# The context's keys laid out by group, and softmax sums spread before they are inverted

## What is computed

```python
# x: (32, 64, 256) after layer norm; ctx: (32, 1601, 256); 16 heads of 16
q = split_heads(x @ Wq.T + bq)
k = split_heads(ctx @ Wk.T + bk)
v = split_heads(ctx @ Wv.T + bv)
score = einsum('bhqd,bhkd->bhqk', q, k) * 4.0
attn = softmax(score, axis=-1)
out = einsum('bhqk,bhkd->bhqd', attn, v) @ Wp.T + bp
```

## Time and profile before

| | us |
|---|---|
| median of three runs | 1734.32 (1733.7 to 1734.82) |
| the profiled execution, its own time | 1735.91 |
| its span, from the first to the last instruction | 1734.1 |
| attention, first scores to last weighting | about 60 to 1240 of the span |
| circuit and feed-forward | about 1240 to 1330 |
| experts | about 1330 to the end |

### The profile page before, as it was taken

The page is one execution under the profiler, slowest core; times in us unless marked ns, Lnnn a source line. Parts: engine busy times, 40 slices in busy tenths (PEclk is TensorE's granted clock), DMA queues, the critical chain, the costliest instruction groups (busy, mean ns, idle before and its releaser), DMA issues. The chain is left out here.

```text
span 1734.1 us, 59228 instructions
## 1 busy us (share of the span) xinstructions
PE 1666.1 (96%) x24340; PEld 1377.8 (79%) x24340; DVE 1425.4 (82%) x3316; ACT 1220.5 (70%) x3297; POOL 948.8 (55%) x1427
## 2 busy tenths in 40 slices
PE   7999999999999999999999999996798899999998
PEld 4777777777777777777777777775577899999998
DVE  5699898998989989898998989888875676767657
ACT  3687788777888778887877878787554365656552
POOL 5265646556465565655556555554310448888850
PEclk9999999999999999999999999996797999999999
DMA  5011111211112111121111111111102356666632
GB/s 177 22 64 46 48 66 42 67 45 53 60 42 68 45 63 50 42 68 45 65 48 45 65 46 64 48 48 57 62 25 86 122 177 228 219 228 219 226 120 103
DMA packets 43439, 147.89 MB, mean 85 GB/s; under 512 B 5680, under 2 KB 25008, under 8 KB 39712
## 3 DMA queue, kind: packets, MB, share of 16 engines
q1 hardware_dynamic: 38416, 130.72, 22.1%
q0 software_dynamic: 4752, 13.38, 2.5%
HBM read 129.79 MB, written 14.16 MB: 83 GB/s over the span
## 5 line engine op out<-in xcount | busy, mean ns | idle before, releaser
L506 ACT ACTIVATE a_probs<-a_probs,a_bias 128x401 f32<-128x401 f32 x1024 | 631.8, 622 | 2.1
L721 DVE TENSOR_SCALAR_CACHE_REDUCE a_probs<-a_pss 128x401 f32<-128x401 f32 x1024 | 526.2, 570 | 56.9 <-PE a_pss L976 42.6
L736 DVE STREAM_TRANSPOSE a_pT<-a_probs 128x1664 f32<-128x1664 f32 x256 | 488.1, 1907 | 61.3 <-PE a_pso L1005 59.8
L976 PE MATMUL a_pss<-a_keys,a_qown 32*32 32x401 f32 x8192 | 273.6, 508 | 2.7 <-issue 1.3
L316 POOL TENSOR_TENSOR a_clo<-a_raw,a_chi 128x416 fp32r<-128x416 f32 x240 | 251.5, 1081 | 0.0
L1005 PEld LDWEIGHTS a_pso<-a_pT,a_v 128*32 128x32 f32 x6656 | 184.5, 112 | 45.7 <-issue 42.8
L1005 PE MATMUL a_pso<-a_pT,a_v 128*32 128x128 f32 x6656 | 202.5, 279 | 3.5 <-ACT a_op L521 2.7
L339 POOL TENSOR_SCALAR a_ex<-a_probs,a_marks 128x4 f32<-128x4 f32 x256 | 75.9, 296 | 220.2 <-ACT a_probs L506 218.1
L1670 PE MATMUL e_psg<-e_xh,e_guh 128*128 128x256 f32 x660 | 189.5, 287 | 5.5 <-DVE e_hl L1416 4.0
L506 ACT ACTIVATION_READ_ACCUMULATOR a_probs<-a_probs,a_bias 128x1 f32 x1024 | 194.5, 190 | 0.0
L1671 PE MATMUL e_psg<-e_xl,e_guh 128*128 128x256 f32 x660 | 186.6, 283 | 0.0
(11 more groups left out here) (253 smaller groups left out, 4288.8 us busy)
## 6 DMA issues: line engine op xcount, KB each, us to landing
a_raw<-in_ctxT SPq DMA_DIRECT2D x60, 832.0 KB, 4.4
f_gur<-in_wgu SPq DMA_DIRECT2D x24, 1408.0 KB, 6.2
f_dr<-in_wd SPq DMA_DIRECT2D x24, 768.0 KB, 4.7
e_big<-ys_scr SPq DMA_DIRECT2D x8, 512.0 KB, 7.0
a_probs<-in_ctxT SPq DMA_DIRECT2D x2, 1664.0 KB, 9.3
a_x<-in_x SPq DMA_DIRECT2D x16, 128.0 KB, 4.4
rows_scr<-f_a SPq DMA_DIRECT2D x8, 256.0 KB, 2.3
rows_scr<-f_a SPq DMA_DIRECT2D x4, 512.0 KB, 3.5
```

Of the source, the lines that this page charges most:

```text
L506: nc.scalar.activation(z, z, ACT.Exp, bias=bias[:, h % 2, at_bias:at_bias + 1], scale=-1.0, accum_out=esum[:, h % 2, j, 2 * e + r:2 * e + ...
L721: nc.vector.tensor_scalar(probs[:, at % RING, j, 0:KG], ps_s[:, j, 0:KG], -SCALE, None, ALU.mult, ALU.min, accum_out=nmax[:, h % 2, at_max ...
L736: nc.vector.transpose(pT[:, turned_slot(h, i)].rearrange("p j k -> p (j k)"), probs[:, at % RING].rearrange("p j k -> p (j k)")).then_inc( ...
L976: mm = nc.tensor.matmul(ps_s[32 * g:32 * g + 32, j, 0:KG], q_own[32 * j:32 * j + 32, n % 2, m, e, 32 * r:32 * r + 32], keys[32 * j:32 * j ...
```

## The change

The host lays each group's keys side by side: group g holds keys g, g+4, g+8, ..., 401 of them in group 0 and 400 in the others (`REAL`), padded to 416. No key is doubled. A key step then multiplies 402 neighbouring columns of the context. The padded length is 13 x 128, and block t of 128 keys for a value step is now every thirteenth column of all four groups, from t on (`t::KT`), 52 bytes apart. Within a group, block t holds keys t, t+13, ..., 31 places of which can be real.

Scores are in the group's own order, so `take_scores` now reads 403 columns in order and writes element (a, t) to place 32t + a of `probs`: neighbouring elements go 128 bytes apart. Columns 400 to 402 of `ps_s` are set once to -1e30 (group 0's scores overwrite the first of them), so that the exponentials of absent keys are 0. `exponentials` works on 13 runs of 31.

The sums need no correction: `less_extra`, `total`, `spread_sums` and `spread` go. POOL lays the 16 sums of each partition on a diagonal (`lay_sums`, 128 x 512), PE multiplies this with a 128 x 32 tile of ones (`totals`, four matmuls of 128 columns right behind `weigh`), DVE inverts all 128 x 128 results into `o_part` (`invert`), and ACT copies the weighted values out in two halves, each times its parity mask. `gather` is as before. The two waits of DVE named above go. In even periods the step of the first quarter moves to the second, and `spread_max` moves behind both steps of the third quarter.

```diff
+KA = 31
+KP = KT * KA
+KM = 402
...
-OWN, DIAG, EXTRA, KEPT, PARITY = slice(0, 2), slice(2, 34), slice(34, 35), slice(35, 36), (slice(36, 68), slice(68, 100))
+REAL = tuple((SK + QK - 1 - g) // QK for g in range(QK))
+ABSENT = -1e30
+OWN, DIAG = slice(0, 2), slice(2, 34)
...
-        plan = [[(n + 1, 2)], [(n + 1, 3), (n + 1, 4)], [(n + 1, 5), (n + 1, 6)], [(n + 1, 7), (n + 1, 8), (n + 1, 9)]]
+        plan = [[], [(n + 1, 2), (n + 1, 3), (n + 1, 4)], [(n + 1, 5), (n + 1, 6)], [(n + 1, 7), (n + 1, 8), (n + 1, 9)]]
...
+        esum, sums_in, ones = sb("a_esum", [P, 2, HALF, 4]), sb("a_sin", [P, HALF, P]), sb("a_ones", [P, 32])
+        o_part = sb("a_op", [P, 2, 4 * SQ])
...
+        by_block = lambda z: z.rearrange("p (t a) -> p t a", a=32)[:, :, 0:KA]
...
-            def less_extra(h, i):
-                at = HALF * h + i
-                e, r = quads(h)[i]
-                pool.wait_ge(exp_done, HALF * (at + 1))
-                if h > 1 and i == 0:
-                    pool.wait_ge(total_filled, h - 1)
-                if at > 0:
-                    pool.wait_ge(sums_ready, at)
-                nc.gpsimd.tensor_scalar(extra[:], probs[:, at % RING, :, KG - 1], mark[:, EXTRA], None, ALU.mult).then_inc(extra_ready, 1)
-                pool.wait_ge(extra_ready, at + 1)
-                nc.gpsimd.tensor_tensor(out=sums[:, h % 2, :, 2 * e + r], in0=esum[:, h % 2, :, 2 * e + r], in1=extra[:], op=ALU.subtract).then_inc(sums_ready, 1)
-            def spread_sums(h):
-                pool.wait_ge(inverse_ready, h + 1)
+            def lay_sums(h):
+                pool.wait_ge(exp_done, HALF * HALF * (h + 1))
                 if h > 0:
-                    pool.wait_ge(sums_filled, h)
-                nc.gpsimd.tensor_tensor(out=sums_in[:].rearrange("p j q b -> p (j q) b"),
-                                        in0=inverse[:].unsqueeze(2).to_broadcast([32, 4 * HALF, 32]),
-                                        in1=mark[0:32, DIAG].unsqueeze(1).to_broadcast([32, 4 * HALF, 32]), op=ALU.mult).then_inc(sums_spread, 1)
+                    pool.wait_ge(totals_filled, h)
+                nc.gpsimd.tensor_tensor(out=sums_in[:].rearrange("p j (q b) -> p (j q) b", b=32),
+                                        in0=esum[:, h % 2].rearrange("p j q -> p (j q)").unsqueeze(2).to_broadcast([P, 4 * HALF, 32]),
+                                        in1=mark[:, DIAG].unsqueeze(1).to_broadcast([P, 4 * HALF, 32]), op=ALU.mult).then_inc(sums_laid, 1)
...
+                if h > 0:
+                    lay_sums(h - 1)
                 if h > 1:
                     gather(h - 2)
-                less_extra(h, 0)
                 if h % 4 == 1 and h > 4:
...
-                less_extra(h, 1)
-                if n + 2 < B:
                     ctx_low(n + 2, k, raw[:])
-                if h > 0:
-                    spread_sums(h - 1)
-                less_extra(h, 2)
                 if k == 1 and n + 2 < B:
                     own_queries(n + 2)
-                less_extra(h, 3)
...
+                if i == 0 and h > 1:
+                    act.wait_ge(sums_laid, h - 1)
                 for j in some:
-                    z = probs[:, at % RING, j, 0:KG]
+                    z = by_block(probs[:, at % RING, j])
                     at_bias = HALF * i + j
                     nc.scalar.activation(z, z, ACT.Exp, bias=bias[:, h % 2, at_bias:at_bias + 1], scale=-1.0,
...
-                act.wait_ge(sums_filled, h + 1)
+                act.wait_ge(inverse_ready, h + 1)
                 if h > 1:
                     act.wait_ge(o_ready, h - 1)
-                nc.scalar.copy(o_part[:, h % 2, :], ps_o[:, 0:2 * P]).then_inc(o_copied, 1)
+                for e in range(2):
+                    last = nc.scalar.activation(o_part[:, h % 2, SQ * e:SQ * (e + 1)], ps_o[:, SQ * e:SQ * (e + 1)], ACT.Identity, scale=mark[:, e:e + 1])
+                last.then_inc(o_copied, 1)
...
-                    dve.wait_ge(sums_ready, at - RING + 1)
                     dve.wait_ge(turned, at - RING + 1)
...
-                    nc.vector.tensor_scalar(probs[:, at % RING, j, 0:KG], ps_s[:, j, 0:KG], -SCALE, None,
+                    nc.vector.tensor_scalar(by_block(probs[:, at % RING, j]).rearrange("p t a -> p a t"), ps_s[:, j, 0:KP].rearrange("p (a t) -> p a t", t=KT), -SCALE, None,
                                             ALU.mult, ALU.min, accum_out=nmax[:, h % 2, at_max:at_max + 1]).then_inc(max_ready, 1)
...
-                dve.wait_ge(total_filled, h + 1)
-                if h > 0:
-                    dve.wait_ge(sums_spread, h)
-                nc.vector.reciprocal(inverse[:], ps_s[0:32, 0, W:W + 4 * HALF]).then_inc(inverse_ready, 1)
+                dve.wait_ge(totals_filled, h + 1)
+                if h > 1:
+                    dve.wait_ge(o_scaled, h - 1)
+                nc.vector.reciprocal(o_part[:, h % 2, P:2 * P], ps_o[:, P:2 * P]).then_inc(inverse_ready, 1)
...
+            dve.wait_ge(q_ready_all, NC * NG)
+            nc.vector.memset(ps_s[:, :, min(REAL):KP], ABSENT).then_inc(absent_set, 1)
...
-                        if h + 1 < NH:
-                            dve.wait_ge(s_filled, HALF * (HALF * (h + 1) + 3) + 1)
                         invert(h - 1)
...
                     m, q = of
                     for k in range(NC):
-                        mm = three(bank[:, 0:W], [w[:, 0, k, m * P:(m + 1) * P] for w in (w_hi, w_lo)],
-                                   [c[:, slot, k].rearrange("p (t g a) -> p g t a", g=QK, a=32)[:, q] for c in (c_hi, c_lo)], k == 0, k == NC - 1)
+                        mm = three(bank[:, 0:KM], [w[:, 0, k, m * P:(m + 1) * P] for w in (w_hi, w_lo)],
+                                   [c[:, slot, k, q * W:q * W + KM] for c in (c_hi, c_lo)], k == 0, k == NC - 1)
                 else:
                     for t in range(of[0], min(of[0] + TILES_A_STEP, KT)):
                         for k in range(NC):
-                            mm = three(bank[:, (t % 2) * D:(t % 2 + 1) * D], [c[:, slot, k, P * t:P * (t + 1)] for c in (c_hi, c_lo)], [w[:, 1, k, :] for w in (w_hi, w_lo)], k == 0, k == NC - 1)
+                            mm = three(bank[:, (t % 2) * D:(t % 2 + 1) * D], [c[:, slot, k, t::KT] for c in (c_hi, c_lo)], [w[:, 1, k, :] for w in (w_hi, w_lo)], k == 0, k == NC - 1)
                 mm.then_inc(kv_filled, 1)
...
-                    pe.wait_ge(q_ready_all, NC * NG)
+                    pe.wait_ge(absent_set, 1)
...
-                        mm = nc.tensor.matmul(ps_s[32 * g:32 * g + 32, j, 0:KG], q_own[32 * j:32 * j + 32, n % 2, m, e, 32 * r:32 * r + 32],
-                                              keys[32 * j:32 * j + 32, m, g * KG:(g + 1) * KG], start=True, stop=True)
+                        mm = nc.tensor.matmul(ps_s[32 * g:32 * g + 32, j, 0:REAL[g]], q_own[32 * j:32 * j + 32, n % 2, m, e, 32 * r:32 * r + 32],
+                                              keys[32 * j:32 * j + 32, m, g * KG:g * KG + REAL[g]], start=True, stop=True)
...
-            def total(h):
-                pe.wait_ge(sums_ready, HALF * (h + 1))
-                pe.wait_ge(max_ready, min(HALF * (HALF * (h + 2) + 2) + 1, HALF * HALF * NH))
-                nc.tensor.matmul(ps_s[0:32, 0, W:W + 4 * HALF], mark[:, DIAG], sums[:, h % 2].rearrange("p j q -> p (j q)"),
-                                 start=True, stop=True).then_inc(total_filled, 1)
-            def spread(h):
-                pe.wait_ge(sums_spread, h + 1)
+            def totals(h):
+                pe.wait_ge(sums_laid, h + 1)
                 for j in range(HALF):
-                    for e in range(2):
-                        mm = nc.tensor.matmul(ps_o[32 * j:32 * j + 32, P + SQ * e:P + SQ * (e + 1)], mark[0:32, PARITY[e]],
-                                              sums_in[:, j, 2 * e:2 * e + 2].rearrange("p q b -> p (q b)"), start=True, stop=True)
-                mm.then_inc(sums_filled, 1)
+                    mm = nc.tensor.matmul(ps_o[32 * j:32 * j + 32, P:2 * P], ones[:], sums_in[:, j, :], start=True, stop=True)
+                mm.then_inc(totals_filled, 1)
...
                 if h > 0:
                     weigh(h - 1)
+                    totals(h - 1)
                 for z in steps[0]:
                     step(*z)
-                if h > 0:
-                    total(h - 1)
                 if h + 1 < NH:
...
-                for z in steps[2][:1]:
+                for z in steps[2]:
                     step(*z)
                 if h + 1 < NH:
                     spread_max(h + 1)
-                for z in steps[2][1:]:
-                    step(*z)
                 if h + 2 < NH:
                     scores(h + 2, 1)
-                if h > 0:
-                    spread(h - 1)
                 for z in steps[3]:
...
-    ctx = np.concatenate([ctx[:, :SK - 1].reshape(B, QK, KG - 1, D), np.broadcast_to(ctx[:, None, SK - 1:], (B, QK, 1, D))], axis=2)
```

(46 more changed lines are left out.)

## The result

The kernel takes 2042.89 us after the change (median of 4 runs, 2041.05 to 2043.16), against 1734.01 us before: a ratio of 1.178, 95% interval 1.177 to 1.180. It is 309 us slower; the forecast was 2040.

The account below looks back on a forecast made before the run. PE bounds the kernel before, DVE after: 16.11 + 5.2 (takes) + 0.76 (inversion) = 22.05, plus 0.6 idle, 22.65 us a period against 17.91; 64 periods add 303 us to 1735.9, said as 2040 us, range 1915 to 2164.

Parts of the forecast that it names:

- So DVE becomes the bound: Steady attention: DVE's work rises from 16.11 to 22.05 us a period, above PE's 17.9; this forecast had 0.74.
- DVE busy for nearly all of a steady window: Sign expected in the steady attention if DVE paced by its writes, with PE busy less or with longer value matmuls.
- Only the loads cost: Rival, chance 0.11: spread writes hidden when the source is PSUM; PE sets 17.3 to 22.4 us a period, up to 2020 us.
- The load: PE's value-step weight loads, columns 52 bytes apart: from no change to 0.13 us more each, 39 a period, 5.1 us.
- The takes: DVE's 403-element writes 128 bytes apart: 0.32 us more each (0.27 to 0.37), 16 a period, 5.2 us.
- The inversion: DVE's reciprocal growing from 16 to 128 elements a partition: 1.00 us, 0.76 more a period; low end 0.15 more.
- `invert`, with the takes queued behind it on DVE, comes two quarters after `totals`: Claim that DVE's inversion asks only for older work, so its new wait was priced at nothing.
- The rest at nothing: Exponentials, ACT's copies, POOL's work, the new waits, moved `spread_max`, memset and marks: no cost a period.
- `spread_max` comes a step later, but the exponentials that need it are a quarter and a take away: Claim that the later spreading of the maximum in the third quarter holds nothing up; priced at nothing.
- Neither costs: faster: Rival, chance 0.10: spread writes and loads run as now, PE saves 0.6 us a period; 1696 us, up to 1725.
- PE's savings: PE, steady attention: shorter key matmuls save 0.16 us and the new sums 0.44, some 0.6 us of 17.9 a period.
- More than both: Rival, chance 0.05: 128-byte steps cost more than 64, or PE's granted clock falls; period over 24.6 us, over 2164 us.

Follow-up runs that it names:

- the variant: Changed kernel with keys in blocks of 32 per group, 416-column key matmuls, neighbouring value loads, 401-element takes in order, new sums, no doubled key: 1758.57 us, ratio 1.014.
- the two last variants: Inversion late and steps as before, no spread access: with 416-column key matmuls 1728.05 us (0.9951), with 402 columns 1719.99 us (0.9913).

## Why the prediction was right in its number, and where it was wrong

**"So DVE becomes the bound" is the step that failed.** PE stayed the bound. The prediction had both engines near one another (22.05 us for DVE, up to 22.4 for PE) and picked DVE, because it took DVE's price in full and leaned only "to the upper half" on the load. The other way round was right: DVE's work is 20.6 us (20.7 where it is the bound), PE's period 22.2 with DVE's writes out of the way. 22.2 and 0.4 of waiting for each other came out where 22.05 and 0.6 of idle had been forecast. The sign that the prediction named for it, DVE busy for nearly all of a steady window, failed too: 91%. So the time is right by luck: another engine's term, near the same size, stood in for the one that failed. The rival "Only the loads cost" had the right bound, with a condition (a hidden write) that did not hold.

**The load** was just above the top of its range: 0.256 us from value matmul to value matmul, 0.136 more, where the bound was 0.13. 39 x 0.136 = 5.3 us on PE's 17.3 make 22.6; measured with DVE out of the way, 22.2. What was said for it, that it is the same memory as DVE's, isn't shown by any run: loads and DVE's writes go alike by step, but a moving operand pays at step 2 already.

On this, the Trainium skill (TensorE: Matmul & The Clock Gate, LDWEIGHTS) gives a time by columns alone. The runs don't agree with that: the same 128 columns took 189 ns at step 1 and 357 at step 13.

**The takes** were over-sized: 0.24 us more, not 0.32, and below the lower bound of 0.27. L1460's 0.80 ns an element, from one instruction of 112 elements, stood for 0.24/403 = 0.60. 16 x 0.08 = 1.3 us of the 1.5 us by which DVE's period came out shorter.

The Trainium skill (SBUF — State Buffer, Door 1: The DMA port swizzle) asks for two hits in each 16-byte line and concludes that a step of four fp32 is free. The runs agree with the two hits (step 2 free at 579 ns) and not with the conclusion (step 4 at 864 ns, step 32 at 830).

**The inversion** took 938 ns (forecast 1.00 us), and 224 with 16 columns: the elements set it. That it costs DVE's time alone was wrong. "`invert`, with the takes queued behind it on DVE, comes two quarters after `totals`" asked whether it waits, not what waits for it: the takes behind it free the score banks late, and PE's scores wait. Moving or shortening it gave 18 to 22 us in the variant without spreading.

**"The rest at nothing"** failed, hidden in this kernel. "`spread_max` comes a step later, but the exponentials that need it are a quarter and a take away" did not hold: ACT waits for it once a period (23.6 us of 600 in the variant, no such row before), and left out were ACT's copies of step results behind that wait, whose banks PE needs. Moving the steps and `spread_max` back gives 26 us there, with the inversion late 30; in the kernel after, where PE's loads cover the rest, both give 6 us. By the same token "Neither costs: faster" (1696 to 1725) would have been 1752.

**PE's savings** of 0.6 us a period were small and are in the sum as said: the key matmul is 9 ns shorter (6 forecast), and between the two last variants the 14 columns gave 8 us (10 forecast).

**"More than both"** stayed away: the granted clock is 0.99 in the steady part, and a step of 128 bytes costs no more than one of 16 or 64.

**Left open:** how much of the 26 us is the step's move and how much that of `spread_max`, and what the kernel would gain without the new wait of `spread_max` for DVE. A load made of four runs of 32 columns, which would let 402-column keys and unspread values stand together, wasn't tried.

## What to carry to other kernels

A layout that makes one reader's operand contiguous moves the step to another reader: price every reader and writer of the buffer, weight loads too, and look where a load has no cover (here 0.117 us, by the prediction's estimate, against 0.12). When two engines come out close, say both periods and give the bound to neither: the time can come out right whichever it is, the cause can't. And an edit that is free behind a bottleneck can cost once that bottleneck goes, so try it in the kernel without the bottleneck as well. Last, a wait that a profile names costs something only if the work behind it starts later than it did: the load ahead of `weigh` waited 0.65 us for DVE in the variant, and `weigh` started no later behind its scores than before.

## What the runs showed that was not expected

- A step of 2 elements costs a weight load (195 against 189 ns) and a DVE write (579 against 578) nothing, but nearly doubles a matmul's pace (0.229 against 0.120 us) where it is the moving operand's.
- A DVE read of PSUM 52 bytes apart is free: 578 ns for 403 elements, as in order.
- The distance adds nothing more: loads of step 13 took 357 ns, of step 26 324.
- The accumulator's read behind a spread take lengthens with it, 0.08 us in the earlier trace rows and 0.15 after.
